# An adaLN block with windowed attention: each step made of two runs of small products and two of whole ones

## The chip, the cores and the metric

One core of one Trainium2 chip runs the whole kernel; the other cores do nothing. The metric is the device time of one execution in microseconds, and lower is better. The kernel before takes 1718.55 us (median of 3 runs, 1714.46 to 1723.47).

## What is computed

The input is 8 sequences of 256 tokens with 128 features. First comes one attention layer (8 heads of 16), and then, on its normalised and modulated output, six layers of the following, which are nearly all of the time:

```python
def attn_layer(x, Wqkv, qs, ksc, Wo):            # HEADS = 16, DIM_HEAD = 64, WINDOW = 32
    q, k, v = split(x @ Wqkv)                    # 128 -> 3 * 1024
    q = l2norm(q) * qs;  k = l2norm(k) * ksc
    q = q * cos * scale + rotate_half(q) * sin * scale
    k = k * cos * inv + rotate_half(k) * sin * inv
    # each window of 32 tokens attends to itself and to the window before it (64 keys), masked
    return local_attention(q, k, v) @ Wo         # 1024 -> 128
def ffn_layer(x, g, bln, W1, b1, W2, b2):        # hidden size 341
    xn = layernorm(x) * g + bln
    a, gate = split(xn @ W1 + b1)
    return a * gelu(gate) @ W2 + b2
for i in range(6):
    x = attn_layer(shift_tokens(x), ...) + x
    x = ffn_layer(shift_tokens(x), ...) + x
```

## The kernel before, in words

The six layers of eight sequences make 48 steps (`SLOTS`), one for each sequence of each layer. Every engine has its own program, an order written out by hand in a function `slot(g)` that it runs once for each step g; semaphores (`wait_ge` and `then_inc`) tie the engines together, and nothing reorders the work. A step's 256 tokens are two halves m = 0 and 1 of 128 tokens, and its 16 heads are two groups g = 0 and 1 of 8.

For one half the work goes round the engines so. TensorE projects Q, K and V (`q`, `k`, `v`; each six products of 128 x 128 by 512 columns, L717 to L721, with weights and input split in a high and a low part). VectorE multiplies Q and K with the tables (`rope_products`, L1420 and L1424), ScalarE squares them (`square_of`, L1063), VectorE sums the squares (`norms`, L1434), ScalarE makes the inverse norms (`inverse_norms`), GpSimd adds the two products (`rotate`, L406) and scales them (`scale`, L415). TensorE turns the result, that is, transposes it (`turn_q` and `turn_k`, 16 small products at L603 each), ScalarE copies it out of PSUM (`copy_q` and `copy_k`, L1081 and L1090), and TensorE makes the scores of each group (`scores`: 4 products at L760 for the mask and 64 at L767). VectorE subtracts the maximum (`centre`, L1445 and L1449), ScalarE takes the exponential (`exps`, L1104), TensorE turns P (`turn_p`), ScalarE copies it (`copy_p`, L1110), TensorE attends (`attend`, 64 products at L802 for a group), VectorE normalises (`normalise`, L1457 and L1460), TensorE turns the output (`turn_o`), ScalarE copies it (`copy_o`, L1119), and `project_out` (L824) is the product with Wo. V goes by `copy_v` (L1096) into `v_nat` and from there by eight DMAs of a half (`move_v`, L333), issued by SyncE, into the windows' places in `v_sb`; two more (`carry_v`, L343) carry the last window over. The feed-forward part of a sequence is done in the three steps behind it (`mean` L831, `variance` L836, gates and values at L846 to L848, `down` L885), with ScalarE's `gates` (L1154, between two table loads) and VectorE's `products` (L1486), `subtract_mean` (L1475) and `add` (L1494).

TensorE's products are of two kinds. The whole ones use all 128 rows and 128 columns of the array. The small ones use a part of it, by `tile_position`: the turns 64 x 128, the mask's 64 x 64, the scores and `attend` 64 x 32. PSUM has 8 banks of 512 floats, used here as four pairs (`pair_of_banks`), and each result lies in a pair until VectorE or ScalarE has read it, so that most of TensorE's waits are for a pair to come free. In the kernel before, P of a half is turned, copied and attended in the half-step of its own scores, with the copies of P group by group (`turn_p(g, 0, 0)`, `turn_p(g, 0, 1)`) and whole products put between them to cover what they wait for. So TensorE's step has eight runs of small products and eight of whole ones.

Steps 0 to 2 have no feed-forward part; steps 3 to 46 are a loop; step 47 and the rest of the last sequences are written out.

## Time and profile before

| what | value |
|---|---|
| time of the kernel before, median of 3 | 1718.55 us (1714.46 to 1723.47) |
| the profiled execution's own time | 1714.33 us |
| its span (first to last instruction) | 1712.5 us |
| busy: TensorE, VectorE, ScalarE, GpSimd | 1615.4, 1338.5, 1282.9, 1067.0 us |
| granted TensorE clock, mean over the span | 0.979 |
| steps 3 to 46, from the first scores of step 3 to those of step 47 (281.40 to 1649.10 us) | 1367.70 us |

The profile is of one execution. Busy time is the union of an engine's instructions, and matmuls overlap: one that takes 0.39 us is followed by the next after 0.23 us, so what a product costs is read as the distance from its start to the next one's start. In the timelines below, a row is a run of like instructions: start, time from its first start to its last end, engine, line, shapes and count; a bracket gives the idle time ahead of it and what ended it.

### The profile page before, as it was taken

Reading aid. Unit: us, or ns where it says so; the run is one execution under the profiler, and the core shown is the slowest. Engines: PE = TensorE matmul, PEld = TensorE weight load, DVE = VectorE, ACT = ScalarE, POOL = GpSimd, SP = SyncE. Lnnn points to the kernel's source line nnn. Section 1 sums busy time; section 2 is a strip of 40 time slices with the busy share of each in tenths; the row PEclk is TensorE's granted clock in tenths of the full one; section 3 lists DMA queues with packets and bytes.
Section 4 is the critical chain, followed back from the end, with each engine's and each line's share of the span. In section 5 each row is a group of like instructions: output and inputs, shape, how many; then the busy total and the mean of one; then the engine's idle time right before and its main releaser. Section 6 shows DMA issues by size and latency. Waiting matters only on the chain.

```text
span 1712.5 us, 89332 instructions
## 1 busy us (share of the span) xinstructions
PE 1615.4 (94%) x36892; PEld 1251.8 (73%) x36892; DVE 1338.5 (78%) x1952; ACT 1282.9 (75%) x2104; POOL 1067.0 (62%) x783
## 2 busy tenths in 40 slices
PE   7897688999999999999999999999999999999986
PEld 3575567777777777777777777777777777777765
DVE  5576767787888888888888888887887878888862
ACT  4795456788777778877778777778777787777763
POOL 2202556578666778667668667578676676676740
PEclk9898799999999999999999999999999999999998
DMA  3000323222323222324222324233223222232220
GB/s 119 2 0 1 73 59 105 62 66 61 91 70 93 70 69 68 85 55 116 68 57 63 88 69 112 51 72 80 72 66 103 70 70 70 69 73 69 71 48 26
DMA packets 75728, 116.79 MB, mean 68 GB/s; under 512 B 17294, under 2 KB 27276, under 8 KB 74764
## 3 DMA queue, kind: packets, MB, share of 16 engines
q1 hardware_dynamic: 75660, 115.99, 27.2%
q8 instruction: 30, 0.49, 0.1%
q14 instruction: 38, 0.31, 0.1%
HBM read 19.04 MB, written 1.05 MB: 12 GB/s over the span
## 4 chain that ended last, share of the span: by engine, by line
PE 89%; issue 5%; ACT 3%; DVE 2%; DMA 0%; ACTq 0%; DVEq 0%; SPq 0%
PE ps L603 15%; PE ps L824 10%; PE ps L717 10%; PE ps L802 9%; PE ps L767 9%; PE ps L721 8%; PE ps L720 8%; PE ps L885 4%; PE ps L760 3%; PE ps L846 2%; PE ps L847 2%; PE ps L848 2%; PE ps L836 2%; PE ps L831 2%; PE ps L592 1%
## 5 line engine op out<-in xcount | busy, mean ns | idle before, releaser
L415 POOL TENSOR_TENSOR arena<-arena,rnorm 128x1024 f32<-128x1024 f32 x192 | 361.9, 1906 | 342.7 <-ACT rnorm L1074 342.7
L406 POOL TENSOR_TENSOR arena<-arena 128x1024 f32<-128x1024 f32 x192 | 457.0, 2380 | 20.8 <-DVE arena L1424 17.9
L603 PEld LDWEIGHTS ps<-cst,arena 64*128 64x128 f32 x6656 | 243.5, 140 | 144.7 <-issue 136.0
L603 PE MATMUL ps<-cst,arena 64*128 64x64 f32 x6656 | 300.6, 230 | 21.6 <-ACT arena L1104 9.4
L1420 DVE TENSOR_TENSOR arena<-ps,rope 128x1024 f32<-128x1024 f32 x192 | 234.7, 1222 | 90.4 <-issue 81.5
L1110 ACT ACTIVATE arena<-ps 128x512 f32<-128x512 f32 x192 | 114.7, 597 | 174.4 <-PE ps L603 174.2
L1424 DVE TENSOR_TENSOR arena<-ps,rope 128x1024 f32<-128x1024 f32 x192 | 233.3, 1215 | 0.0
L721 PE MATMUL ps<-wqkv_hi,x_hi 128*128 128x512 f32 x576 | 230.1, 399 | 0.0
L720 PE MATMUL ps<-wqkv_lo,x_hi 128*128 128x512 f32 x576 | 229.2, 398 | 0.0
L717 PE MATMUL ps<-wqkv_hi,x_lo 128*128 128x512 f32 x576 | 215.7, 456 | 12.8 <-issue 11.6
L1434 DVE TENSOR_REDUCE norm<-arena 128x16 f32<-128x1024 f32 x192 | 224.3, 1209 | 0.0
L1445 DVE TENSOR_REDUCE rmax<-ps 128x8 f32<-128x512 f32 x192 | 131.9, 687 | 105.9 <-PE ps L767 105.3
L1063 ACT ACTIVATE arena<-ps 128x1024 f32<-128x1024 f32 x192 | 190.4, 1020 | 11.7 <-DVE arena L1424 11.7
L802 PE MATMUL ps<-v_sb,arena 64*32 64x66 f32 x12288 | 166.3, 227 | 23.1 <-issue 7.5
L824 PE MATMUL ps<-arena,wo_sb 128*128 128x256 f32 x768 | 186.3, 385 | 1.2 <-issue 1.2
L802 PEld LDWEIGHTS ps<-v_sb,arena 64*32 64x32 f32 x12288 | 138.6, 106 | 60.4 <-issue 50.0
L767 PE MATMUL ps<-k_t,arena 64*32 64x64 f32 x12288 | 166.2, 225 | 7.1 <-issue 7.1
L767 PEld LDWEIGHTS ps<-k_t,arena 64*32 64x32 f32 x12288 | 134.3, 106 | 31.1 <-issue 8.2
L824 PEld LDWEIGHTS ps<-arena,wo_sb 128*128 128x128 f32 x768 | 138.6, 190 | 19.7 <-issue 1.3
L1090 ACT ACTIVATE k_t<-ps 128x1024 f32<-128x1024 f32 x96 | 98.4, 1025 | 71.9 <-PE ps L603 70.1
L1449 DVE TENSOR_TENSOR arena<-ps,rmax 128x512 f32<-128x512 f32 x192 | 132.8, 692 | 15.2 <-DVE rmax L1445 0.7
L1460 DVE TENSOR_TENSOR arena<-ps,rden 128x512 f32<-128x512 f32 x192 | 132.9, 692 | 14.8
(122 smaller groups left out, 2752.3 us busy)
## 6 DMA issues: line engine op xcount, KB each, us to landing
v_sb<-v_nat SPq DMA_DIRECT2D x576, 130.0 KB, 2.4
v_sb<-v_nat SPq DMA_DIRECT2D x192, 65.0 KB, 2.0
wqkv_sb<-wqkv SPq DMA_DIRECT2D x6, 1536.0 KB, 6.4
v_sb<-v_sb SPq DMA_DIRECT2D x96, 65.0 KB, 2.0
wo_sb<-wo SPq DMA_DIRECT2D x6, 512.0 KB, 3.8
w_sb<-w SPq DMA_DIRECT2D x6, 341.0 KB, 3.0
x<-xT SPq DMA_DIRECT2D x1, 1024.0 KB, 5.0
scl<-scales SPq DMA_DIRECT2D x6, 128.0 KB, 6.2
```

What stands on the lines that cost most here:

```text
L406: pool.tensor_tensor(t_cos[:, m, j, :], t_cos[:, m, j, :], t_sin[:, j, :], ALU.add)\
L415: pool.tensor_tensor(x, x, rnorm[:, H * j:H * j + H].unsqueeze(2).to_broadcast([P, H, D]), ALU.mult).then_inc(s[done], 1)
L603: mm = pe.transpose(ps[0:width, bank + t, 64 * c:64 * c + 64], src[r], ident[r, r], tile_position=(64 * t, 0))
L717: pe.matmul(ps[:, bank + c, :], x_lo[:, m, :], wqkv_hi[:, w], start=True, stop=False)
L720: pe.matmul(ps[:, bank + c, :], x_hi[:, m, :], wqkv_lo[:, w], start=False, stop=False)
L721: mm = pe.matmul(ps[:, bank + c, :], x_hi[:, m, :], wqkv_hi[:, w], start=False, stop=True)
L767: mm = pe.matmul(ps[W * w:W * w + W, 4 * g + c, SPAN * hh:SPAN * hh + SPAN], q_t[r, 4 * g + hh, W * w:W * w + W], k_t[r, 4 * g + hh, P * m ...
L802: mm = pe.matmul(ps[W * w:W * w + W, 4 - 2 * g + c, ON * hh:ON * hh + ON], p_t[r, h, W * w:W * w + W], v_sb[r, m, w, VD * h:VD * h + ON], ...
L824: mm = pe.matmul(ps[:, 0, 0:N], wo_sb[:, c, :], o_t[:, c, :], start=(c == 0), stop=(c == H // 2 - 1), skip_group_check=True)
L1420: dve.tensor_tensor(t_cos[:, m, j, :].rearrange("p (h d) -> p h d", h=H), src.rearrange("p a (h d) -> p (a h) d", h=8), tc.unsqueeze(1).to ...
L1424: dve.tensor_tensor(t_sin[:, j, :].rearrange("p (h s d) -> p h s d", h=H, s=2), src.rearrange("p a (h s d) -> p (a h) s d", h=8, s=2)[:, : ...
L1434: dve.tensor_reduce(norm2[:, H * j:H * j + H], sq[:, j, :].rearrange("p (h d) -> p h d", h=H), AX.X, ALU.add).then_inc(s["normed"], 1)
```

## The change

Each of TensorE's steps becomes four runs: small, whole, small, whole. P is turned one half-step behind its scores and attended two behind: the small run at the head of step g holds `turn_q(g, 0)`, `attend(g - 1, 0, ...)`, `turn_k(g, 0)`, `turn_p(g - 1, 1)`, `scores(g, 0, ...)` and `turn_o(g - 1, 0)`. The run in the middle holds the same one half-step on. P of a half is turned in one piece (16 products for 2 times 8) and copied by one ScalarE instruction of 1024 columns for two of 512. The feed-forward part moves by a step at its head: mean and variance of sequence f are taken in step f + 2, not f + 1, while its gates stay in step f + 3. Every result has a new pair of banks (the tables `Q_PAIR` to `A_PAIR`), and with it new waits. ScalarE, VectorE, GpSimd and SyncE get new orders to match, and the head and the end of the pipeline are written anew. No product is added or removed.

The diff, cut to its core (of the slots of TensorE, ScalarE and VectorE only the lines of the new one are shown):

```diff
             def slot(g, norm=True, ahead=True, more=True, after=None, layer=None):
                 f = g - 2
-                if norm:
-                    divide(f)
                 scale(g, 1)
                 if ahead:
                     rotate(g + 1, 0, 0)
+                    low(g + 1, 1)
+                    rotate(g + 1, 0, 1)
                     if after == 7:
+                        table(layer, 1)
                         split_weights(layer, 2)
-                    low(g + 1, 1)
+                    scale(g + 1, 0)
+                    if after == 6:
+                        table(layer, 0)
                 if norm:
+                    divide(f)
                     scale_norm(f)
                 if ahead:
-                    rotate(g + 1, 0, 1)
-                    if after == 6:
-                        table(layer, 0)
-                    scale(g + 1, 0)
+                    rotate(g + 1, 1, 0)
                     if after == 6:
                         split_weights(layer, 0)
-                    rotate(g + 1, 1, 0)
-                    if after == 6:
-                        split_weights(layer, 1)
-                    if more:
-                        low(g + 2, 0)
                 if norm:
                     rest(f)
                 if ahead:
-                    rotate(g + 1, 1, 1)
-                    if after == 6:
-                        table(layer, 1)
                     if after == 2:
                         split_up(layer)
+                    if more:
+                        low(g + 2, 0)
+                    if after == 6:
+                        split_weights(layer, 1)
+                    rotate(g + 1, 1, 1)
...
+        Q_PAIR, K_PAIR, V_PAIR = (1, 0), (2, 3), (1, 0)
+        QT_PAIR, KT_PAIR, PT_PAIR, OT_PAIR = (1, 3), (2, 1), (2, 1), (3, 2)
+        S_PAIR = ((2, 0), (3, 1))
+        A_PAIR = ((0, 3), (0, 0))
...
+            def turn_k(pair, m, ff=True):
                 n = 2 * pair + m
                 pe.wait_ge(s["k_scaled"], CREDIT + n + 1)
+                if m == 0:
+                    pe.wait_ge(s["att_done"], CREDIT + pair - 1)
+                elif ff:
                     pe.wait_ge(s["f_prod"], CREDIT + 3 * (pair - LAG) + 3)
                 else:
+                    q_read(n + 1)
...
+            def turn_q(pair, m, ff=True):
                 n = 2 * pair + m
                 pe.wait_ge(s["q_scaled"], CREDIT + n + 1)
+                if m == 0:
+                    pe.wait_ge(s["v_copied"], CREDIT + n + 1)
+                elif ff:
+                    pe.wait_ge(s["f_gated"], CREDIT + 3 * (pair - LAG) + 3)
+                    pe.wait_ge(s["f_centred"], CREDIT + pair - 1)
+                else:
+                    pe.wait_ge(s["o_copied"], CREDIT + n - 2)
...
+            def attend(pair, m, g, bank=None):
                 n = 2 * pair + m
                 if g == 0:
                     pe.wait_ge(s["v_moved"], CREDIT + 16 * (18 * pair + 8 + 10 * m))
-                    pe.wait_ge(s["p_copied"], CREDIT + 2 * n + 2)
-                    pe.sem_inc(s["pe_waited"], 1)
-                elif over_q:
-                    pe.wait_ge(s["roped"], CREDIT + 4 * n + 10)
-                    pe.wait_ge(s["squared"], CREDIT + 2 * n + 5)
-                    pe.sem_inc(s["pe_waited"], 1)
+                    pe.wait_ge(s["p_copied"], CREDIT + n + 1)
+                if bank is None:
+                    bank = 2 * A_PAIR[m][g]
+                    if m:
+                        if g == 0:
+                            pe.wait_ge(s["v_copied"], CREDIT + n + 3)
+                        else:
+                            pe.wait_ge(s["o_normed"], CREDIT + 2 * n + 1)
+                    elif g == 0:
+                        q_read(n + 3)
+                        pe.wait_ge(s["f_done"], CREDIT + pair - 2)
+                    else:
+                        k_read(n + 3)
+                        pe.wait_ge(s["f_log"], CREDIT + pair - 1)
+                pe.sem_inc(s["pe_waited"], 1)
...
+            def slot(g, att=True, norm=True, ff=True, ahead=True):
+                turn_q(g, 0)
+                if att:
+                    attend(g - 1, 0, 0)
+                turn_k(g, 0)
+                if att:
+                    attend(g - 1, 0, 1)
+                    turn_p(g - 1, 1)
                 scores(g, 0, 0)
+                scores(g, 0, 1, att=att)
+                if att:
+                    turn_o(g - 1, 0)
                 if ahead:
                     q(g + 1, 0)
                 if ff:
+                    gates_01(g - LAG)
                 if ahead:
+                    k(g + 1, 0)
                 if ff:
+                    gate_2(g - LAG)
+                v(g, 1)
+                if ff:
+                    values(g - LAG, ahead)
+                if norm:
+                    pe.wait_ge(s["f_gated"], CREDIT + 3 * (g - LAG) + 3)
+                    mean(g - 2, 6)
+                if att:
+                    attend(g - 1, 1, 0)
+                turn_q(g, 1, ff)
+                turn_k(g, 1, ff)
+                turn_p(g, 0)
+                if att:
+                    attend(g - 1, 1, 1)
                 scores(g, 1, 0)
                 scores(g, 1, 1)
+                if att:
+                    turn_o(g - 1, 1)
                 if ahead:
+                    if not att:
+                        pe.wait_ge(s["v_copied"], CREDIT + 2 * g + 2)
                     q(g + 1, 1)
                     k(g + 1, 1)
+                    if norm:
+                        pe.wait_ge(s["centred"], CREDIT + 4 * g + 4)
+                        variance(g - 2, 2)
+                    if att:
+                        project_out(g - 1)
+                    if norm:
+                        pe.wait_ge(s["f_log"], CREDIT + g - 1)
+                    v(g + 1, 0)
+                    if ff:
+                        q_read(2 * g + 3)
+                        down(g - LAG)
...
+            def slot(g, att=True, shifted=True, norm=True, ff=True, ahead=True, more=True, after=None, layer=None):
+                copy_q(g, 0)
+                copy_k(g, 0)
+                if att:
+                    copy_p(g - 1, 1)
+                inverse_norms(g, 1)
+                if shifted:
+                    shift(g - 2)
+                if att:
+                    copy_o(g - 1, 0)
+                exps(g, 0, 0)
+                exps(g, 0, 1)
                 if ff:
                     act.preload_act_table_set("gelu_and_others")
+                    gate(g - LAG, 0, ps[:, 7, 0:N], 1)
+                    gate(g - LAG, 1, ps[:, 7, N:2 * N], 1)
+                if ahead:
+                    square_of(g + 1, 0, 0)
+                if ff:
+                    gate(g - LAG, 2, ps[:, 6, 0:N], 2)
+                copy_v(g, 1)
+                if ahead:
+                    high(g + 1, 1)
+                    square_of(g + 1, 0, 1)
+                copy_q(g, 1)
+                copy_k(g, 1)
+                copy_p(g, 0)
+                if ff:
                     act.preload_act_table_set("natural_log_exp_and_others")
                 if after == 7:
                     round_weights(layer, 2)
+                if att:
+                    copy_o(g - 1, 1)
                 if ahead:
                     inverse_norms(g + 1, 0)
                 exps(g, 1, 0)
                 if norm:
+                    square(g - 2)
+                exps(g, 1, 1)
                 if after == 6:
                     round_weights(layer, 0)
                 if after == 2:
                     round_up(layer)
                 if ahead:
                     square_of(g + 1, 1, 0)
+                    if norm:
+                        inverse_deviation(g - 2)
                     square_of(g + 1, 1, 1)
+                    if after == 6:
+                        round_weights(layer, 1)
+                    copy_v(g + 1, 0)
+                    if more:
+                        high(g + 2, 0)
+                    if norm:
+                        round_norm(g - 2)
...
+            def slot(g, att=True, norm=True, ff=True, ahead=True, first_mean=False):
+                if att:
+                    normalise(g - 1, 0, 0)
+                    normalise(g - 1, 0, 1)
                 centre(g, 0, 0)
                 centre(g, 0, 1)
                 if ahead:
                     rope_products(g + 1, 0, 0)
                     rope_products(g + 1, 0, 1)
                 if ff:
+                    product(g - LAG, 2, ps[:, 2, 0:N], 1)
+                if norm:
+                    subtract_mean(g - 2)
+                if ff:
+                    product(g - LAG, 0, ps[:, 3, 0:N], 2)
+                    product(g - LAG, 1, ps[:, 3, N:2 * N], 2)
+                if att:
+                    normalise(g - 1, 1, 0)
                 if ahead:
                     norms(g + 1, 0)
+                if att:
+                    normalise(g - 1, 1, 1)
                 centre(g, 1, 0)
                 centre(g, 1, 1)
                 if ahead:
                     rope_products(g + 1, 1, 0)
                     rope_products(g + 1, 1, 1)
+                    if att:
+                        residual(g - 1)
+                    if ff:
+                        add(g - LAG)
+                    if first_mean:
+                        subtract_mean(0, 5)
                     norms(g + 1, 1)
```

How the order moves on TensorE, in the loop over steps 3 to 46. Before, around the turning of P of the first half, there stood (L603 is a turn, L824 Wo's product, L846 a feed-forward product, and the other rows are instructions of the sequencer that wait or count):

```order
L777 ISA
L780 REGISTER_ALU [waits centred]
L603 MATMUL ps<-cst,arena 128x64 [waits exped]
L603 MATMUL ps<-cst,arena 128x64 x7
L824 MATMUL ps<-arena,wo_sb 128x256 x4
L603 MATMUL ps<-cst,arena 128x64 [waits p_copied,exped]
L603 MATMUL ps<-cst,arena 128x64 x7
L862 REGISTER_ALU
L846 MATMUL ps<-f_hi,w1_lo 128x256 [waits f_gated]
```

Each turn of a group of P stood between whole products. Now the head of the loop's step reads (L623 is a turn, L864 `attend`):

```order
L623 MATMUL ps<-cst,arena 128x64 [waits q_scaled,v_copied]
L623 MATMUL ps<-cst,arena 128x64 x15
L843 ISA
L844 ISA [waits v_moved]
L749 ISA [waits p_copied]
L750 ISA [waits roped]
L854 REGISTER_ALU [waits squared]
L864 MATMUL ps<-v_sb,arena 32x66 [waits f_done]
L864 MATMUL ps<-v_sb,arena 32x66 x31
```

The turn of Q and `attend` of the step before now follow each other, and `attend` has six semaphores to wait for. (One row of a fp32 product in these lists is two matmuls in the profile, except for the turns.)

On VectorE, in the loop, the rows around the middle of a step were the following before the change: `norms` (L1434) of the next step's first half behind `normalise` (L1457, L1460) of this one's.

```order
L1457 RECIPROCAL rden<-ps 128x8 [waits attended]
L1459 REGISTER_ALU [waits recip]
L1460 TENSOR_TENSOR arena<-ps,rden 128x2x4x64 [waits o_turned]
L1457 RECIPROCAL rden<-ps 128x8 [waits attended]
L1460 TENSOR_TENSOR arena<-ps,rden 128x2x4x64 [waits o_turned,recip]
L1432 REGISTER_ALU
L1433 REGISTER_ALU [waits squared]
L1434 TENSOR_REDUCE norm<-arena 128x16 [waits logged]
L1432 REGISTER_ALU
L1434 TENSOR_REDUCE norm<-arena 128x16 [waits logged,squared]
```

Now `norms` (L1533) stands between the two groups of `normalise` (L1557, L1560), and these are of the step before:

```order
L1557 RECIPROCAL rden<-ps 128x8 [waits attended]
L1559 REGISTER_ALU [waits recip]
L1560 TENSOR_TENSOR arena<-ps,rden 128x2x4x64 [waits o_turned]
L1531 REGISTER_ALU
L1532 REGISTER_ALU [waits squared]
L1533 TENSOR_REDUCE norm<-arena 128x16 [waits logged]
L1531 REGISTER_ALU
L1533 TENSOR_REDUCE norm<-arena 128x16 [waits logged,squared]
L1536 TENSOR_SCALAR norm<-norm 128x32 [waits normed]
L1553 REGISTER_ALU
L1557 RECIPROCAL rden<-ps 128x8 [waits attended]
L1560 TENSOR_TENSOR arena<-ps,rden 128x2x4x64 [waits o_turned,recip]
```

The second `normalise` of a half, which `turn_o` waits for, now has `norms` ahead of it, and `norms` waits for ScalarE's square of K.

## Rows read from the trace of the kernel before

**Rows 1.** The page: busy time of the engines, and the chain that ended last.

```profile
PE 1615.4 (94%) x36892; PEld 1251.8 (73%) x36892; DVE 1338.5 (78%) x1952; ACT 1282.9 (75%) x2104; POOL 1067.0 (62%) x783
...
PE 89%; issue 5%; ACT 3%; DVE 2%; DMA 0%; ACTq 0%; DVEq 0%; SPq 0%
```

**Rows 2.** Windows: length, then busy of PE, PEld, DVE, ACT, POOL, and PE's clock.

```profile
907.56:938.20 30.64, 30.42 (x740) 24.01 (x737) 25.29 (x36) 25.04 (x40) 27.29 (x20) 1.00 0.28 65
281.40:1649.10 1367.70, 1342.59 (x32388) 1057.83 (x32384) 1127.58 (x1585) 1076.62 (x1734) 956.12 (x690) 1.00 0.30 75
184.40:281.40 97.00, 82.18 (x2117) 63.94 (x2116) 71.42 (x94) 58.22 (x95) 59.42 (x41) 0.90 0.27 64
1649.10:1712.50 63.40, 42.48 (x764) 34.23 (x760) 20.97 (x44) 27.16 (x46) 9.06 (x10) 0.89 0.12 33
```

**Rows 3.** Timeline of TensorE over one step of the loop.

```profile
906.92 0.71 PE L603 MATMUL ps<-cst,arena 64*128 64x64 f32 x16
907.56 0.30 PE L760 MATMUL ps<-mask_bf,ident_bf 64*64 64x256 bf16 x4
...
909.68 0.73 PE L717 MATMUL ps<-wqkv_hi,x_lo 128*128 128x512 f32 x2
...
914.89 0.39 PE L720 MATMUL ps<-wqkv_lo,x_hi 128*128 128x512 f32 x1
915.12 0.40 PE L721 MATMUL ps<-wqkv_hi,x_hi 128*128 128x512 f32 x1
915.45 0.46 PE L603 MATMUL ps<-cst,arena 64*128 64x64 f32 x8
915.84 1.99 PE L824 MATMUL ps<-arena,wo_sb 128*128 128x256 f32 x8
917.76 0.46 PE L603 MATMUL ps<-cst,arena 64*128 64x64 f32 x8
918.15 0.39 PE L846 MATMUL ps<-f_hi,w_lo 128*128 128x256 f32 x1
918.37 0.28 PE L847 MATMUL ps<-f_lo,w_hi 128*128 128x256 f32 x1
918.49 0.28 PE L848 MATMUL ps<-f_hi,w_hi 128*128 128x256 f32 x1
...
919.41 1.72 PE L802 MATMUL ps<-v_sb,arena 64*32 64x66 f32 x128
921.06 1.20 PE L603 MATMUL ps<-cst,arena 64*128 64x64 f32 x32
922.19 0.74 PE L717 MATMUL ps<-wqkv_hi,x_lo 128*128 128x512 f32 x2
...
931.81 0.70 PE L831 MATMUL ps<-f_a,cst 128*128 128x256 f32 x2
932.62 1.82 PE L802 MATMUL ps<-v_sb,arena 64*32 64x66 f32 x128
```

**Rows 4.** Timeline of ScalarE: a table load, and two reads of 1024 columns.

```profile
910.01 1.28 ACT L1160 ACT_TABLE_LOAD   x1
...
918.76 1.94 ACT L1063 ACTIVATE arena<-ps 128x1024 f32<-128x1024 f32 x2
```

**Rows 5.** The same in step 11, where ScalarE's loop over layers turns back.

```profile
539.06 1.28 ACT L1160 ACT_TABLE_LOAD   x1 [2.47 <-issue]
```

**Rows 6.** VectorE over one step (the first is `rope_products`, the second `norms`).

```profile
L1420 DVE TENSOR_TENSOR arena<-ps,rope 128x1024 f32<-128x1024 f32 x4 | 4.9, 1222 | 1.8 <-issue 1.8
...
L1434 DVE TENSOR_REDUCE norm<-arena 128x16 f32<-128x1024 f32 x4 | 4.7, 1208 | 0.0
```

**Rows 7.** SyncE: eight issues of one `move_v`; then the page on their landing.

```profile
909.83 4.99 SPq L333 DMA_DIRECT2D v_sb<-v_nat  x8
...
v_sb<-v_nat SPq DMA_DIRECT2D x576, 130.0 KB, 2.4
```

**Rows 8.** TensorE in its loop's first pass, around a stop.

```profile
285.36 0.66 PE L767 MATMUL ps<-k_t,arena 64*32 64x64 f32 x30 [2.13 <-issue]
```

More of the change, by code:

```diff
@@ L958, in _ @@
+            mean(0, 5)
+            k_read(2 * LAG + 1)
+            variance(0, 6)
             with pe.Fori(LAG, SLOTS - 1) as g:
                 slot(pe.snap(g))
[L960 to L967 removed]
@@ new lines, in _ @@
+            project_out(g - 1)
+            pe.wait_ge(s["o_normed"], CREDIT + 4 * g + 1)
+            turn_p(g, 1, 6)
+            turn_o(g, 0, 2)
+            down(g - LAG)
+            pe.wait_ge(s["att_done"], CREDIT + g)
+            attend(g, 1, 0, 4)
+            attend(g, 1, 1, 6)
+            pe.wait_ge(s["f_done"], CREDIT + g - 2)
+            mean(g - 1, 1)
+            pe.wait_ge(s["f_log"], CREDIT + g - 1)
+            pe.wait_ge(s["o_copied"], CREDIT + 2 * g + 1)
+            last_up(g - 2)
@@ L975, in _ @@
+            turn_o(g, 1, 4)
+            variance(g - 1, 1)
+            project_out(g, 6)
+            down(g - 2, 7)
+            mean(g, 4)
+            variance(g, 4)
+            pe.wait_ge(s["f_log"], CREDIT + g)
+            last_up(g - 1)
+            pe.wait_ge(s["att_done"], CREDIT + g + 1)
+            last_up(g)
+            pe.wait_ge(s["f_done"], CREDIT + g - 1)
+            down(g - 1, 7)
+            pe.wait_ge(s["f_log"], CREDIT + g + 1)
+            down(g, 4)
         @block.scalar
```

455 lines of the change are left out of this document (196 added, 259 removed).

## The prediction

> **What bounds the kernel now.** The page comes first. TensorE is busy for 94% of the span, and the chain that ended last runs over it for 89%, with 5% more of "issue" [rows 1]. The windows say where: in steps 3 to 46, which take 1367.7 of the 1712.5 us, it is idle for 25.1 us in all, at a granted clock of 1.00 [rows 2]. The other engines have room: in the step from 907.56 to 938.20 us VectorE is busy for 25.3 of 30.64 us, ScalarE for 25.0 and GpSimd, in this one with weights to split, for 27.3 [rows 2]. So a step is worth what TensorE's products cost, start to start. The 44 steps would take 44 x 30.64 = 1348 at this length and take 1368. The 20 more are stops of about 2 us in the loop's first pass, of which one is shown [rows 8], and at ends of ScalarE's loops [rows 5]. Head and tail are another matter: TensorE is idle for 14.8 of the 97 us of steps 0 to 2 and for 21 of the last 63.4 us [rows 2].
>
> **What a change of kind costs.** The timeline of TensorE shows it to 0.01 us [rows 3]. Whole products follow each other after 0.23 us (914.89 to 915.12), but the last one before a turn holds 0.33 (915.12 to 915.45): 0.10 more. A whole product of the feed-forward part holds 0.12 (918.37 to 918.49), the first one behind a turn 0.22 (918.15 to 918.37): 0.10 more again. Eight turns take 0.39 (915.45 to 915.84) and 32 take 1.13 (921.06 to 922.19), so one costs 0.031 and each run of turns 0.14 on top. From one whole run to the next, over a run of turns, the fixed part is thus 0.34.
>
> **TensorE's new step.** Before, it has eight whole runs and eight blocks of turns (P's two, K's and Q's as one, the output's, for each half). Now it has two whole runs, and six blocks of turns: four in the first small run, where `attend` stands between them, and two in the second, where Q, K and P are turned side by side. The sum by difference: six whole runs fewer at 0.20 is 1.2, two blocks of turns fewer at 0.14 is 0.3. Besides, TensorE waits no more between `mean` and `attend` (931.81 to 932.62 is 0.81, where two of Wo's products and a change of kind cost 0.53), which gives 0.3. 30.64 - 1.8 = 28.85. The sum by parts agrees. A block of 16 turns is 0.14 + 16 x 0.031 = 0.64; a group of `attend` is half of 1.65 (919.41 to 921.06), 0.82; a half's scores are 2.12 (907.56 to 909.68). The first small run is 4 x 0.64 + 2 x 0.82 + 2.12 = 6.3, the second 0.82 + 1.62 + 0.82 + 2.12 + 0.64 = 6.0. Wo's products cost (1.92 - 0.20) / 8 = 0.215 each (915.84 to 917.76). The whole runs are 18 x 0.235 + 18 x 0.12 + 2 x 0.215 + 0.2 = 7.0 (Q, K, V, gates, values, mean) and 18 x 0.235 + 24 x 0.215 + 0.2 = 9.6 (Q, K, V, variance, Wo, down). Together 28.9.
>
> One thing speaks against so much. A block of 16 turns with the mask's products behind it takes 0.64 (906.92 to 907.56 [rows 3]), just what the slope and the 0.14 give for one with whole products behind it: for a run of turns the next small shape is as dear as a whole one. Counted by shape (turns, mask, scores and `attend`, whole), a step changes 26 times before and still 20 times now. The Trainium skill ("TensorEngine Tiling (Array Packing)", Key Properties) says that a change of the tiling mode, though not of the tile, drains TensorE; by that rule, with which the 0.64 agrees, a small run is no single piece and only the six fewer changes would count. The sum above goes by the rows; the other count is the first rival.
>
> **What TensorE will wait for.** I walk through a step, with t = 0 at `turn_q(g, 0)`. Reads of 1024 columns are 0.97 apart and end 1.02 after their start; a table load is 1.28 [rows 4]. The products with the tables take 2 x 1.14 for Q or K, the two sums of `norms` 2.4 [rows 6].
> - First small run, 0 to 6.3. The copy of K starts behind `turn_k` at 2.2 and ends at 3.2; the scores start at 3.56. Covered by 0.3. `attend(g - 1, 0, 0)` waits for `add`, which follows `down` of the step before: about 0.1.
> - First whole run, to 13.3. VectorE starts its step 3.1 late, since `add` and `norms(g, 1)` run over; it centres from 5.0 to 7.8 and multiplies Q by 10.2. ScalarE does the exponentials by 8.5, a table load, two gates, and the square of Q by 11.7; `values` waits for that at 11.8: 0.1.
> - Second small run, to 19.3. `mean` ends at 13.4, `subtract_mean` at 13.9, and both products of the feed-forward part at 14.7, which `turn_k(g, 1)` needs at 14.6: 0.1. ScalarE copies Q and K from 14.9 to 16.9, and the scores are due at 16.6: 0.2. `norms(g + 1, 0)` holds VectorE from 15.5 to 18.1, so `normalise(g - 1, 1, 1)` ends at 19.1, and `turn_o(g - 1, 1)` is due at 18.8: 0.3.
> - Second whole run, 9.6 long: VectorE multiplies K by 26.3, ScalarE squares it by 27.4, and `copy_v(g + 1, 0)` is done when `down` is. Nothing.
> That is 0.7 to 0.8, and the step 29.65. GpSimd, in this walk, scales K of a half 6 us before its turn. The V moves: eight issues take 5.0 and land 2.4 later [rows 7]; those of half 0 start at 3.0, land at 10.5 and are needed at 11.9.
>
> The gain of a step is 30.64 - 29.65 = 1.0, and 44 steps give 44. Bounds: no wait at all gives 1.8 and 79; waits of twice what I find give 0.25 and 11.
>
> **Head, tail and the stops.** Steps 0 to 2 take 97.0 us [rows 2], latency for the most part, since there P goes round within its half-step. The new step 0 attends nothing, and in steps 1 and 2 the round trips lie behind other work; VectorE then sets the pace with some 24 us of work. I take 26.3, 26.5 and 26.5, and add 2.1 for a stop and 2 for mean and variance of sequence 0, which stand by themselves: 83.4, and 14 gained (bounds 0, if code loading takes the gain, and 20). The tail is a chain through every engine, the same from the last scores on. It has more straight code, one `attend` of 256 matmuls more, hence one stop of 2 more; on the other side the last scores come about 5 earlier. I take 3 gained (bounds -6 and 8). The 2.47 us at ScalarE's loop end [rows 5] now delay the copies of Q and K with 0.3 of cover; four of these cost some 1.6 to 2.2 each, as now, and the rounding of weights is better hidden: 2 gained.
>
> The sum is 44 + 14 + 3 + 2 = 63. Against the profiled execution's own 1714.3 this is 1651; the median of the plain runs stands 4 above it, and I put the forecast between, at 1653.
>
> **Rivals.**
> - Every change of shape costs alike. The fixed 0.34 of a round trip over turns is two changes, 0.17 each; six fewer are 1.0 and the wait 0.3, 1.3 for 1.8. With my waits 0.55 a step is left, 24, and with head and tail 1714 - 43 = 1671. Against it: the 0.20 of a whole run is seen at the whole products themselves, and they are what goes. Chance 0.1. (This is the case of the Trainium skill's tiling page, Key Properties.)
> - More waits of the kind that I found, two or three tenths in several places, since the covers are thin: 1.5 a step, 0.3 gained, 1714 - 13 - 19 = 1682. Chance 0.15.
> - No change: the waits take all of 1.8, and the head gives little. 1706 to 1722. Chance 0.06.
> - Slower, by one mechanism: the DMAs of V. `copy_v(g, 1)` needs all eight DMAs of half 0 landed, and in ScalarE's order the square of K and the copies of Q and K stand behind it, for which the second scores wait. They now start only after `attend(g - 1, 0, 1)`. With 1.4 of slack, each further us of landing is one of TensorE's. At 7.4 us from first issue to last landing it is hidden; beyond 8.8 it costs, and from about 10.2 on it has used up step and head (1.0 + 19 / 44 = 1.4). At 12 the step is 32.85, 2.2 longer than now: 1714 + 97 - 19 = 1792. For it speaks that the queue is shared with the weights; against it that the median landing is 2.4 [rows 7]. Chance 0.07.
> - Almost no waits, 28.9 to 29.2 a step: about 1620. Chance 0.1.
>
> **How the numbers follow.** My forecast, a step of 29.2 to 30.0 us, 1635 to 1671, has 0.52. The range takes in its bounds, the almost free case and the two of less gain: 1620 to 1692 holds 0.82. Within 0.5% (about what a measurement of this kernel can tell from no change) is 1710 to 1727. Faster by more has 0.52 + 0.1 + 0.15 + 0.1 = 0.87, less 0.01 for the edge; the same has 0.06, slower 0.07 and the 0.01 of the other edge.
>
> **What would show it.** In the new timeline the step of the loop is 29.65 long; the last whole product of a run still holds 0.33, the first 0.10 too much, twice a step each; the four waits are found at `values`, `turn_k(g, 1)`, the second scores and `turn_o(g - 1, 1)`, none over 0.5; scores of step 3 start near 266 us. The prediction is wrong if the boundary inside a small run (turn to `attend`, six semaphores to read) costs more than a turn's 0.14, if the granted clock, 1.00 in steps 3 to 46 and 0.90 in steps 0 to 2 with their gaps [rows 2], falls in the longer small runs, or if a wait of over 1 us stands in the step.

## The result, and the profile after

The changed kernel takes 1738.8 us (1737.7 to 1743.0), the kernel before 1717.6 (1714.5 to 1723.5): ratio 1.0124, interval 1.0091 to 1.0156. It is slower by 1.2%, where I forecast 1653. The page of after, its head, the busy times and the chain:

```profile
span 1741.1 us, 89711 instructions
PE 1578.5 (91%) x36892; PEld 1278.8 (73%) x36892; DVE 1380.0 (79%) x1952; ACT 1284.1 (74%) x2008; POOL 1070.1 (61%) x783
...
PE 76%; issue 10%; DVE 10%; ACT 3%; DVEq 1%; DMA 0%; POOL 0%; ACTq 0%; SPq 0%; POOLq 0%
```

TensorE's share of the chain fell from 89% to 76%, and VectorE, with 2% before [rows 1], has 10%. The windows of after answer to [rows 2]: one step, steps 3 to 46, steps 0 to 2, and the part from the first scores of step 47 on.

```profile
979.80:1011.08 31.28, 29.49 (x739) 24.43 (x736) 26.82 (x37) 24.22 (x37) 20.59 (x16) 1.00 0.27 64
281.04:1667.49 1386.45, 1307.76 (x32384) 1082.95 (x32385) 1165.99 (x1582) 1078.32 (x1646) 958.33 (x688) 0.99 0.29 72
183.04:281.04 98.00, 77.26 (x1953) 61.70 (x1954) 71.86 (x91) 54.27 (x83) 60.12 (x41) 0.90 0.28 73
1667.49:1741.05 73.56, 50.58 (x934) 41.60 (x930) 24.09 (x52) 30.91 (x51) 9.78 (x11) 0.82 0.16 43
```

TensorE's own work in steps 3 to 46 did fall, from 1342.6 to 1307.8 us busy. But it is idle for 78.7 us there, where it was for 25.1. The list of its waits names the new one:

```profile
PE ps L808 <- DVE arena L1560: 40.1, 33, 1.3
...
PE ps L864 <- DVE h L1590: 9.2, 44, 0.3
```

The second scores of half 0 (those of its second group of heads; L808 is their mask) wait 33 times, 1.2 us each, for VectorE's `normalise(g - 1, 0, 0)`. The timelines of VectorE and GpSimd at a step's end say why that is late (the last two rows are the masks of the first and the second scores):

```profile
1007.41 0.48 DVE L1590 SCALAR_TENSOR_TENSOR h<-ps,par,h 128x256 f32 x1 [2.26 <-PE ps L947]
1007.81 2.34 DVE L1533 TENSOR_REDUCE norm<-arena 128x16 f32<-128x1024 f32 x2
1010.18 2.17 DVE L1536 TENSOR_SCALAR norm<-norm 128x32 f32<-128x32 f32 x1
1012.27 0.20 DVE L1557 RECIPROCAL rden<-ps 128x8 f32<-128x8 f32 x1
1012.59 0.69 DVE L1560 TENSOR_TENSOR arena<-ps,rden 128x512 f32<-128x512 f32 x1
...
1009.39 0.41 POOL L418 TENSOR_TENSOR x_lo<-h,x_hi 64x128 fp32r<-64x128 f32 x1 [0.18 <-POOL x_lo L415]
1009.96 2.36 POOL L425 TENSOR_TENSOR arena<-arena 128x1024 f32<-128x1024 f32 x1 [0.16 <-POOL x_lo L418]
...
1011.08 0.30 PE L808 MATMUL ps<-mask_bf,ident_bf 64*64 64x256 bf16 x4
1013.43 0.30 PE L808 MATMUL ps<-mask_bf,ident_bf 64*64 64x256 bf16 x4 [1.25 <-DVE arena L1560]
```

L1536 is the floor of the norms, a maximum over 32 columns, the last instruction of `norms`. It lasts 2.17 us, and the same instruction lasts 0.18 elsewhere. GpSimd's sum of K's two parts (L425) begins 0.22 earlier and ends at 1012.32; the floor ends at 1012.35. The record shows no idle time at all: the hold is inside a duration. A shorter hold was in the trace of before as well:

```profile
937.76 0.33 DVE L1437 TENSOR_SCALAR norm<-norm 128x32 f32<-128x32 f32 x1
939.33 0.69 DVE L1445 TENSOR_REDUCE rmax<-ps 128x8 f32<-128x512 f32 x1 [1.24 <-PE ps L767]
...
937.31 0.75 POOL L442 TENSOR_TENSOR f_a<-f_a 128x256 f32<-128x256 f32 x1
```

There the floor ends at 938.09, GpSimd's product at 938.06, and what follows on VectorE waits for scores until 939.33 anyway. The change put a longer instruction of GpSimd at this place, and behind the floor two operations that TensorE waits for. The Trainium skill ("SBUF — State Buffer", Who interferes with whom) says that VectorE and GpSimd share a pair of ports, which whoever starts first has for its whole instruction, and that a `tensor_scalar` can need it while a `tensor_reduce` does not. The rows agree: the two sums before the floor keep their 1.2 us each beside GpSimd's work, and the floor is held to the end of GpSimd's sum.

The hold is not in every step, and after shows by itself what it costs. Ahead of steps 11, 27 and 43 the floor lasts 0.26 to 0.27, and these steps are 29.9 to 30.0 long (19 and 35, behind a floor of 0.27, take 31.1 and 31.2, and 31.0 in the first kernel below, which has no floor at all); ahead of steps 7, 15, 23, 31 and 39 it lasts about 0.6, and they are 30.4 to 30.7; where it lasts 2.1 to 2.2, most are 31.2 to 31.4.

### The profile page after: what moved, and what is told of

The parts are those of the page before. It is cut to its first block, busy times and chain, and to the rows that moved or that the text cites. A ratio compares the mean times of both kernels' runs of the same rounds, so it can differ in the third digit from the quotient of the medians.

```text
span 1741.1 us, 89711 instructions
## 1 busy us (share of the span) xinstructions
PE 1578.5 (91%) x36892; PEld 1278.8 (73%) x36892; DVE 1380.0 (79%) x1952; ACT 1284.1 (74%) x2008; POOL 1070.1 (61%) x783
## 4 chain that ended last, share of the span: by engine, by line
PE 76%; issue 10%; DVE 10%; ACT 3%; DVEq 1%; DMA 0%; POOL 0%; ACTq 0%; SPq 0%; POOLq 0%
PE ps L623 10%; PE ps L888 10%; PE ps L740 9%; PE ps L743 8%; PE ps L744 8%; PE ps L815 7%; DVE norm L1533 5%; PE ps L864 5%; PE ps L947 3%; PE ps L903 3%; PE ps L808 2%; PE ps L905 2%; PE ps L904 2%; DVE arena L1560 2%; PE ps L612 1%
## 5 line engine op out<-in xcount | busy, mean ns | idle before, releaser
L425 POOL TENSOR_TENSOR arena<-arena 128x1024 f32<-128x1024 f32 x192 | 456.2, 2376 | 136.3 <-DVE arena L1523 122.5
L623 PE MATMUL ps<-cst,arena 64*128 64x64 f32 x6656 | 291.0, 230 | 45.7 <-issue 13.9
L623 PEld LDWEIGHTS ps<-cst,arena 64*128 64x128 f32 x6656 | 249.3, 140 | 103.1 <-issue 89.3
L1148 ACT ACTIVATE arena<-ps 128x1024 f32<-128x1024 f32 x192 | 196.9, 1026 | 102.4 <-DVE arena L1523 101.3
L1533 DVE TENSOR_REDUCE norm<-arena 128x16 f32<-128x1024 f32 x192 | 224.5, 1210 | 0.2 <-ACT arena L1148 0.2
L740 PE MATMUL ps<-wqkv_hi,x_lo 128*128 128x512 f32 x576 | 204.7, 437 | 0.6 <-issue 0.6
L864 PE MATMUL ps<-v_sb,arena 64*32 64x66 f32 x12288 | 166.7, 227 | 14.3 <-DVE h L1590 9.2
L888 PE MATMUL ps<-arena,wo_sb 128*128 128x256 f32 x768 | 175.7, 382 | 1.4 <-ACT arena L1204 1.4
L815 PE MATMUL ps<-k_t,arena 64*32 64x64 f32 x12288 | 170.1, 229 | 6.7 <-issue 6.6
L1204 ACT ACTIVATE arena<-ps 128x1024 f32<-128x1024 f32 x96 | 98.5, 1026 | 99.3 <-PE ps L623 99.2
L864 PEld LDWEIGHTS ps<-v_sb,arena 64*32 64x32 f32 x12288 | 136.4, 106 | 42.6 <-issue 36.0
L888 PEld LDWEIGHTS ps<-arena,wo_sb 128*128 128x128 f32 x768 | 147.0, 192 | 22.5 <-ACT arena L1204 1.9
L815 PEld LDWEIGHTS ps<-k_t,arena 64*32 64x32 f32 x12288 | 137.5, 107 | 31.4 <-issue 9.2
L1560 DVE TENSOR_TENSOR arena<-ps,rden 128x512 f32<-128x512 f32 x192 | 132.8, 692 | 14.4
L1166 ACT ACTIVATE arena<-ps 128x1024 f32<-128x1024 f32 x96 | 98.4, 1025 | 45.7 <-PE ps L623 34.0
```

What stands on the lines that cost most here:

```text
L425: pool.tensor_tensor(t_cos[:, m, j, :], t_cos[:, m, j, :], t_sin[:, j, :], ALU.add)\
L623: mm = pe.transpose(ps[0:width, bank + t, 64 * c:64 * c + 64], src[r], ident[r, r], tile_position=(64 * t, 0))
L740: pe.matmul(ps[:, bank + c, :], x_lo[:, m, :], wqkv_hi[:, w], start=True, stop=False)
L815: mm = pe.matmul(ps[W * w:W * w + W, bank + c, SPAN * hh:SPAN * hh + SPAN], q_t[r, 4 * g + hh, W * w:W * w + W], k_t[r, 4 * g + hh, P * m ...
L864: mm = pe.matmul(ps[W * w:W * w + W, bank + c, ON * hh:ON * hh + ON], p_t[r, h, W * w:W * w + W], v_sb[r, m, w, VD * h:VD * h + ON], start ...
L888: mm = pe.matmul(ps[:, bank, 0:N], wo_sb[:, c, :], o_t[:, c, :], start=(c == 0), stop=(c == H // 2 - 1), skip_group_check=True)
```

## The experiments

Each was compared with the kernel before on its chip; the ratios are to it. Where a step's length or a distance between starts is given, it is taken start to start in the trace. In the diffs `...` marks lines left out. All kernels but `x2_sum_waits` and `x9_sum_earlier` are without the floor, by the first diff, which is not shown again.

**Floor taken out** (`x1_no_floor`). Only a norm of nearly zero would come out otherwise.

```
-                dve.wait_ge(s["normed"], CREDIT + 2 * n + 2)
-                dve.tensor_scalar(norm2[:, :], norm2[:, :], 1e-24, None, ALU.max).then_inc(s["guarded"], 1)
...
-                act.wait_ge(s["guarded"], CREDIT + n + 1)
-                act.activation(norml[:, :], norm2[:, :], ACT.Ln, scale=2.0 ** 24)...
+                act.wait_ge(s["normed"], CREDIT + 2 * n + 2)
+                act.activation(norml[:, :], norm2[:, :], ACT.Ln, scale=2.0 ** 24, bias=2.0 ** 24 * 1e-24)...
```

> The changed kernel without VectorE's floor of the norms (a maximum over 32 columns, the last instruction of VectorE's loop); ScalarE's Ln gets 1e-24 as a bias instead. In 35 of 45 steps of after this instruction lasts 2.1 to 2.2 us instead of 0.18, and ends together with a sum of GpSimd's that began 0.2 us before it (1009.96 to 1012.32 there, 1010.18 to 1012.35 here). Theory H, held off by GpSimd: the instruction waits for GpSimd's sum to end, both normalise operations and the second scores of the step stand behind it, and the step is 31.3 instead of 29.9. Without it nothing holds VectorE: the wait of 1.2 before the second scores goes, a step is 29.9 to 30.1, 35 x 1.4 = 49 are gained: 1690 (1684 to 1700). Rival L, the end of VectorE's loop: its branch costs 2 us before the next instruction can start, and the record of the last one is stretched over it. Then the 2 us appear between the last sum of norms and the first reciprocal, and the time is 1737 to 1741. Rival D, VectorE simply has too much to do behind add: a gain of 0.2 a step, 1732.

Measured: 1688.0 us, ratio 0.9857 (0.9838 to 0.9875). The step is 29.90. VectorE and TensorE of this kernel at the same place:

```profile
977.96 2.34 DVE L1534 TENSOR_REDUCE norm<-arena 128x16 f32<-128x1024 f32 x2
980.22 0.20 DVE L1556 RECIPROCAL rden<-ps 128x8 f32<-128x8 f32 x1
...
981.24 0.30 PE L808 MATMUL ps<-mask_bf,ident_bf 64*64 64x256 bf16 x4
981.47 0.86 PE L815 MATMUL ps<-k_t,arena 64*32 64x64 f32 x64
982.26 0.30 PE L808 MATMUL ps<-mask_bf,ident_bf 64*64 64x256 bf16 x4
```

The reciprocal follows the sums at once, across the same loop end, so the 2 us were not that end (rival L falls), and the second mask starts 1.02 behind the first, where in after it was 2.35. The floors of over 2 us are 33 in after's loop and not the 35 that I had counted.

**The floor kept, GpSimd's sum behind it** (`x2_sum_waits`).

```
+                    pool.wait_ge(s["guarded"], CREDIT + 2 * g + 4)
                     rotate(g + 1, 1, 1)
```

> The changed kernel with one wait more: GpSimd begins its last sum of a step (cosine and sine part of K) only once VectorE has done the floor of the norms. The floor stays where it is, and no work is left out. Theory H: in after GpSimd's sum starts 0.2 us ahead of the floor; now it starts about 0.3 us later, after it, and the floor lasts 0.18 again. Gain as without the floor, less a little: 1690 to 1702, steps of 29.9 to 30.2. Rival L (end of VectorE's loop): nothing changes for VectorE, 1739 or slower. Rival D (too much work): 1739 too.

Measured: 1691.5 us, ratio 0.9892 (0.9865 to 0.9919), steps of 29.9 to 30.0.

```profile
980.02 0.18 DVE L1537 TENSOR_SCALAR norm<-norm 128x32 f32<-128x32 f32 x1
...
980.37 2.36 POOL L425 TENSOR_TENSOR arena<-arena 128x1024 f32<-128x1024 f32 x1 [0.73 <-DVE norm L1537]
```

One wait more, on an engine with room, and nothing left out: the floor is back at 0.18, and 47 us are gone. VectorE has the same instructions in the same order as in after, so rival D falls too.

**GpSimd's sum earlier** (`x9_sum_earlier`), a smaller hold.

```
                     rotate(g + 1, 1, 0)
+                    if more:
+                        low(g + 2, 0)
+                    rotate(g + 1, 1, 1)
...
                     rest(f)
-                    if more:
-                        low(g + 2, 0)
...
-                    rotate(g + 1, 1, 1)
```

> The changed kernel with the floor, and with GpSimd's last sum of a step put ahead of rest(f); the lower part of x stays ahead of it. Nothing is added or left out. The sum, 2.36 long, then begins about 1.2 us earlier in after's times (1008.8 instead of 1009.96) and ends at 1011.2, while the floor still begins at 1010.2. Theory H (VectorE's floor is held until GpSimd's sum ends): the floor lasts 1.0 to 1.2 instead of 2.17. A hold of 2.0 cost 1.4 a step, so some 0.6 are covered; a hold of 0.9 costs 0.3 to 0.4, a step is 30.2 to 30.4, and 35 x 1.0 are gained: 1704 (1696 to 1712). Rival L (the end of VectorE's loop): 1739, and the floor stays at 2.1 to 2.2.

Measured: 1707.3 us, ratio 0.9959 (0.9945 to 0.9973).

```profile
991.61 1.23 DVE L1536 TENSOR_SCALAR norm<-norm 128x32 f32<-128x32 f32 x1
...
990.43 2.37 POOL L425 TENSOR_TENSOR arena<-arena 128x1024 f32<-128x1024 f32 x1 [0.16 <-POOL x_lo L418]
```

With the floor at 0.18, 1.23 and 2.17 us a step is 29.9, 30.4 and 31.3. So the step follows the length of the hold, as theory H has it.

**The kernel before without the floor** (`x3_before_no_floor`), with the diff of the first.

> The kernel before, without the floor in the same way. There the floor takes 0.33 to 0.66 us in most steps and 1.47 in each eighth, but VectorE's next work is a maximum over scores that TensorE delivers only 1.2 us later. Theory H: no gain, 1716 to 1719: the hold of GpSimd was there before, hidden behind the wait for the scores, and the change has brought it on the path. If the floor cost something before too, it is at most 5 x (1.47 - 1.2) = 1.4 us.

Measured: 1715.0 us, ratio 1.0009 (0.9996 to 1.0022), steps of 30.7 as before. The hold was hidden.

**An extra whole run** (`x7_extra_boundary`).

```
-                if att:
+                if att and not ahead:
                     turn_o(g - 1, 1)
...
                     q(g + 1, 1)
+                    if att:
+                        turn_o(g - 1, 1)
```

> The changed kernel without the floor, and with one block of 16 turns (the output of half 1) moved from the end of the second small run into the whole run behind it, after Q's products. The number of blocks of turns stays, one whole run more is made. By the prediction's price a whole run's boundaries cost 0.20: 44 x 0.20 = 9 us more than x1_no_floor, 1697. By the price of the first rival (every change of shape 0.17) nearly the same, 7.5. If boundaries cost nothing, 1688. What it could add by itself: the copy of this block on ScalarE comes 1.9 later, and with it the exponentials of half 1; if that reaches TensorE, it is more than 15.

Measured: 1741.7 us, ratio 1.0138 (1.0110 to 1.0166): 54 more than `x1_no_floor`, not 9. A step is 1.48 longer.

```profile
1001.75 0.40 PE L744 MATMUL ps<-wqkv_hi,x_hi 128*128 128x512 f32 x1
1002.08 0.71 PE L623 MATMUL ps<-cst,arena 64*128 64x64 f32 x16
1002.72 0.73 PE L740 MATMUL ps<-wqkv_hi,x_lo 128*128 128x512 f32 x2
...
1003.99 0.39 PE L744 MATMUL ps<-wqkv_hi,x_hi 128*128 128x512 f32 x1
1005.35 0.67 PE L898 MATMUL ps<-f_a,cst 128*128 128x256 f32 x2 [0.96 <-ACT f_a L1220]
...
1002.83 1.02 ACT L1207 ACTIVATE arena<-ps 128x1024 f32<-128x1024 f32 x1 [2.20 <-PE ps L623]
...
1004.80 0.40 ACT L1220 ACTIVATE f_a<-f_a 128x256 f32<-128x256 f32 x1
```

The boundaries cost 0.30: 0.10 before the block (1001.75 to 1002.08), 0.11 behind it, and 0.09 where scores now meet a whole product. The other 1.2 is one wait: `variance` (L898) waits for a square on ScalarE (L1220), which stands behind the copy of the moved block (L1207). By the term that it was made to test it should have been 9. The expectation had named the late copy as what could make it more than 15, and had not priced it; so the total says nothing on the boundaries, and only the distances between starts do.

**Turns of Q and K side by side** (`x5_turns_together`).

```
                 turn_q(g, 0)
+                turn_k(g, 0)
                 if att:
                     attend(g - 1, 0, 0)
-                turn_k(g, 0)
-                if att:
                     attend(g - 1, 0, 1)
```

> The changed kernel without the floor, with TensorE's turns of Q and K side by side in the first small run: turn_q, turn_k, attend, attend, turn_p in place of turn_q, attend, turn_k, attend, turn_p. No work is added or left out. In x1_no_floor a step is 29.90, and TensorE's starts show 0.12 more at a turn followed by attend, 0.135 more at attend followed by a turn, and a further 0.27 at the first attend (it waits for add, behind down of the step before). Theory W (the step is TensorE's work and a few small waits): the wait for add goes, since the turn of K lies before it, and two changes of kind go, less 0.08 for the step from Q's turns to K's: 0.4 to 0.5 a step, 44 x 0.45 = 20, so 1668 (1664 to 1674). Rival V (VectorE sets the step behind add): its first normalise starts no earlier, and the time stays at 1686 to 1690.

Measured: 1674.4 us, ratio 0.9772 (0.9731 to 0.9813), a step of 29.63: 0.27 gained where 0.45 was expected. The small run in `x1_no_floor`, and then here:

```profile
977.28 0.71 PE L623 MATMUL ps<-cst,arena 64*128 64x64 f32 x16
978.19 0.85 PE L864 MATMUL ps<-v_sb,arena 64*32 64x66 f32 x64 [0.20 <-DVE h L1589]
978.98 0.71 PE L623 MATMUL ps<-cst,arena 64*128 64x64 f32 x16
979.62 0.86 PE L864 MATMUL ps<-v_sb,arena 64*32 64x66 f32 x64
980.59 0.72 PE L623 MATMUL ps<-cst,arena 64*128 64x64 f32 x16
```

```profile
972.28 1.21 PE L623 MATMUL ps<-cst,arena 64*128 64x64 f32 x32
973.42 1.80 PE L864 MATMUL ps<-v_sb,arena 64*32 64x66 f32 x128
975.33 0.71 PE L623 MATMUL ps<-cst,arena 64*128 64x64 f32 x16
```

The two blocks of turns and the first wait went from 0.91 + 0.64 to 1.14, as said. But the two groups of `attend` take 1.91 from their start to the next turn, where 0.79 and 0.98 stood: the 0.14 that the turns gain beyond the wait of 0.27 is lost again at the joint of two groups of the same shape. Two changes of shape fewer gained nothing in sum.

**The straight parts.** Five kernels change only head or tail: `x4_head_order` has V's copy ahead of K's square in steps 0 to 2, on the kernel without the floor; `x6_both_orders` has the same on `x5_turns_together`; `x10_first_norm` puts the norm of sequence 0 into step 2, also on `x5_turns_together`; `x8_tail_order` has `variance` behind the first `attend` of step 47, on the kernel without the floor, and `x11_best` has that on `x10_first_norm`. First `x4_head_order`:

```
+                    if not ff:
+                        copy_v(g + 1, 0)
                     square_of(g + 1, 1, 1)
...
-                    copy_v(g + 1, 0)
+                    if ff:
+                        copy_v(g + 1, 0)
```

> The changed kernel without the floor, and in steps 0 to 2 alone ScalarE copies V of the next step ahead of the square of K (in after it stands behind it). In these steps TensorE has no products of Wo and down, and its first turn of a step waits for this copy: 3.83 us at 209.49, 1.17 at 244.95, 2.58 at 280.17. Theory, the head is set by this chain (product of K with the tables on VectorE, its square, the copy of V, the turn of Q): 1.0 to 1.4 us earlier in each of three steps, 3 to 4 us less than the kernel without the floor. Rival, the head is set by loading code (the page puts these waits down to issue): no difference between the two.

Measured: 1684.5 us, ratio 0.9862 (0.9819 to 0.9905). Here and in `x1_no_floor` the first turn of step 1 starts 0.1 behind the copy of V, and TensorE's stop ahead of it fell from 3.99 to 1.74. Steps 0 and 1 fell from 30.45 to 28.10 and from 34.87 to 33.48, and step 2 rose from 32.30 to 34.07. The scores of step 3 come 2.6 earlier, 0.7 of it from ahead of step 0; the total can't be told from `x1_no_floor`.

The same on the other order, `x6_both_orders`:

> The order of x5_turns_together, and the order of ScalarE's copy of V in steps 0 to 2 of x4_head_order. If the two add up, 3 to 4 us less than x5_turns_together: 1665. If step 2 gives back what step 0 gains, as scores of step 3 only 2.6 earlier in x4_head_order say, 1 to 3 less.

Measured: 1676.7 us, ratio 0.9774 (0.9750 to 0.9798). The stop ahead of the first turn of step 1 fell here too, from 3.66 to 1.52, but steps 0 to 2 take 98.5 where they took 98.0 in `x5_turns_together`: nothing is left of the 3 us.

The norm of sequence 0, `x10_first_norm` (TensorE's part; the other engines' orders of step 2 change with it):

```
...
-            with pe.Fori(1, LAG) as g:
-                slot(pe.snap(g), norm=False, ff=False)
-            mean(0, 5)
-            k_read(2 * LAG + 1)
-            variance(0, 6)
+            slot(1, norm=False, ff=False)
+            slot(2, ff=False)
...
```

> As x5_turns_together, and the norm of sequence 0 is made inside step 2, as in every later step, in place of by itself behind step 2 (steps 1 and 2 of TensorE are written out for it). In x1_no_floor variance(0) waits 1.74 for its square at 274.44, and mean, variance and this wait stand alone: about 3 us of the 97.6 of the head. If the head is what its open waits and its work add up to, scores of step 3 come 2.5 to 3.5 earlier, at 277.5 to 278.5, and the time is 1671. If the first turns then wait for VectorE instead (scores of step 3 at 280 or later, as in x6_both_orders), 1674.

Measured: 1676.3 us, ratio 0.9776 (0.9756 to 0.9796). It misses its 1671, and neither of its two cases came: steps 0 to 2 take 103.5 instead of 98.0, and step 3 takes 33.4 instead of 36.2. With the steps written out, TensorE's stops of 1 to 2 us that the trace puts down to "issue" stand in steps 1 and 2 (1.97 at 267.54, 1.94 at 284.86), and fewer in step 3 than in `x5_turns_together`. `x11_best` has the same head and takes 100.2.

The tail, `x8_tail_order`:

```
-            variance(g - 2, 0)
             pe.wait_ge(s["centred"], CREDIT + 4 * g + 3)
             attend(g, 0, 0, 6)
+            variance(g - 2, 0)
```

> The changed kernel without the floor; in the straight part behind the last step alone the first attend of step 47 stands before the variance of sequence 45, for whose square TensorE waits 2.0 us at the end of the last small run. The attend needs only P, long turned, and the centring of the scores just made. If the part behind the last scores is bound by TensorE's order, 0.8 to 1.2 us less than x1_no_floor: 1687. If its chain runs over the exponentials and the turn of P (3 us later), nothing: 1688. A difference this small may not be told from none in the total; the start of the turn of P in the trace tells it.

Measured: 1688.3 us, ratio 0.9830 (0.9801 to 0.9860). From the last scores to the turn of P behind them it is 10.4 us, and 10.7 without the order: no gain that the total shows.

And `x11_best`, with both:

> As x10_first_norm, with the order of x8_tail_order in the part behind the last step. 0 to 1 us less than x10_first_norm: 1670 to 1671, ratio to before 0.974.

Measured: 1674.7 us, ratio 0.9759 (0.9733 to 0.9784). It can't be told from `x5_turns_together`, which has less in it. Both beat the kernel before by 2.3 to 2.4%, and by the ratios the changed kernel by 3.5 to 3.6%. Both are without the floor; the order of `x5_turns_together` with the floor kept and GpSimd made to wait was not run.

## Why the prediction was wrong

In the loop the change does nearly what I said, and that is lost by one instruction, which my walk had left out. Without it the kernel takes 1688.0 us, which is still 35 above the forecast: head and tail gained nothing. By parts, in us of the span (steps by their first scores):

| | before | forecast | after | no floor |
|---|---|---|---|---|
| up to step 0 | 184.4 | 184.4 | 183.0 | 183.8 |
| steps 0 to 2 | 97.1 | 83.4 | 98.0 | 97.6 |
| step 3 | 37.0 | | 41.6 | 36.8 |
| steps 4 to 46 | 1330.7 | | 1344.8 | 1297.3 |
| steps 3 to 46 | 1367.7 | 1321.7 | 1386.4 | 1334.1 |
| from step 47 | 63.4 | 60.4 | 73.6 | 69.4 |
| whole span | 1712.5 | 1649.9 | 1741.1 | 1684.9 |

- **The step that failed** is the walk's first item: "VectorE starts its step 3.1 late, since `add` and `norms(g, 1)` run over". With t = 0 at 1007.13, the sums of `norms` end at 1010.15, 3.0 later, where I had 3.1. VectorE then starts its step at 1012.27, 5.1 late. I had priced `norms` by its two sums [rows 6] and left out its third instruction. I looked at GpSimd only for what it delivers ("GpSimd, in this walk, scales K of a half 6 us before its turn"), and never for what it holds. Shown by the three lengths of the hold, of which the one at 0.18 has the floor kept, and by the kernel before, where the same instruction costs nothing. Worth 1344.8 - 1297.3 = 47.5 us, of 91 between the forecast's span and after's. It is also the wait of over 1 us that I had named as a sign of being wrong; the other two did not come (a turn with `attend` behind it costs no more than I had, and the granted clock is 1.00 in the step and 0.99 over steps 3 to 46).
- **TensorE's new step**: right, within 0.1. Without the floor the four runs take 6.63, 7.14, 6.50 and 9.61, 29.9 in all, where I had 6.3, 7.0, 6.0 and 9.6 without waits. The waits below make up the difference. Scores take 2.04 where I had 2.12, and a group of `attend` 0.79 where I had 0.82; 48 turns side by side take 1.85 where I had 1.63, since 0.14 and 0.09 pass at the joints of Q's, K's and P's turns, which I had for free. 16 turns with `attend` behind them take 0.64, as I had it. An extra whole run costs 0.30 (`x7_extra_boundary`), where I had 0.20. The rival by which every change of shape costs alike is not borne out: the joints of blocks of one shape (0.14 and 0.09) cost about as much as that from turns to `attend` (0.15), and in `x5_turns_together` two changes fewer gained nothing in sum. What passes at a joint stays open.

```profile
961.18 0.87 PE L864 MATMUL ps<-v_sb,arena 64*32 64x66 f32 x64
962.13 1.92 PE L623 MATMUL ps<-cst,arena 64*128 64x64 f32 x48
963.97 0.86 PE L864 MATMUL ps<-v_sb,arena 64*32 64x66 f32 x64
965.00 0.30 PE L808 MATMUL ps<-mask_bf,ident_bf 64*64 64x256 bf16 x4 [0.16 <-issue]
```

- **The waits**: 0.7 to 0.8 forecast, 1.0 found: attend for `add` 0.27, turn of P 0.18, turn of Q 0.15 (961.18 to 962.13 is 0.95 for a group of 0.79), scores of half 1 0.23, and about 0.17 at `values`. The step is 29.90 where I had 29.65, so this term, the waits, was 0.25 too small: 44 x 0.25 = 11 us. `turn_o(g - 1, 1)` shows no wait in most steps, and a turn of P takes its place. The waits behind an `attend` (0.08 to 0.16 of idle) come with no engine late in the trace; what they are stays open.
- **Head**: "The new step 0 attends nothing, and in steps 1 and 2 the round trips lie behind other work" failed. I took 26.3 to 26.5 a step, and they take 32.0, 33.7 and 32.3. TensorE's work fell (77.3 busy, 82.2 before), and its idle time rose from 14.8 to 20.7. VectorE's work was 24.0 a step, as said, but it idles for 26 us, so it does not set the pace. One link is the chain of K's product, its square, V's copy and the turn of Q: `x4_head_order` and `x6_both_orders` shorten its wait by some 2 us, and the next steps give it back in part or whole. Which chain sets steps 1 and 2 is not settled. Worth 14.6 us.
- **Tail**: "the last scores come about 5 earlier" failed. From the first scores of step 47 to the last it is 16.5 and 18.2 us in the two traces of the old order, 20.0 to 22.9 in nine of the new one, and 18.2 and 15.2 in `x11_best` and `x10_first_norm`. More work is not the reason: up to the mask of the last scores TensorE is busy for 11.5 us in `x10_first_norm`, at a granted clock of 1.00, and for 13.9 in before. What fills the time are stops that the trace puts down to "issue", 6.9 us in after and 2.0 in before, and the clock, 0.85 in after and 1.00 in before. The forecast had one such stop of 2 for all of it. What the stops are stays open. From the last scores on, the old order takes 46.9 and 48.6, seven kernels of the new one without the hold 46.1 to 48.5, which is the same, as said; but `x9_sum_earlier` takes 49.3, and `x10_first_norm`, `x11_best` and after take 53.3, 50.7 and 50.7, at a clock of 0.78 to 0.81. Worth 13 us in after, and 9 without the floor.
- **First pass of the loop**: 41.6 in after and 36.8 without the floor. In after's step 3 whole products start 0.43 apart in two stretches instead of 0.23, behind stops of 1.5 and 1.8 us; the mean granted clock is 0.75, and 0.91 without the floor. Of kernels that begin alike one had 0.79 and took 39.9 (`x8_tail_order`), and others had 0.91 to 0.95, so these 5 us may be chance.
- **The rivals**: the one on the slower side was the wrong one. No wait in after's list of waits is for V's DMAs. None of my cases has GpSimd in it, and 0.08 for slower was too little for a schedule with covers of 0.2 to 0.3.

## What to carry to other kernels

An order of work changes which instructions of VectorE and GpSimd run at the same time, and here a short `tensor_scalar` that began behind a long `tensor_tensor` of GpSimd's lasted until that one's end: look, in the trace of before, for instructions of one shape whose duration differs (here 0.18, 0.33 and 1.47), and ask who will stand beside and behind them afterwards. A wait inside a duration shows in no list of waits; the spread of a line's durations gives it away (the floor before: 0.18 at least, 0.19 in the middle, 1.48 at most). If such a pair is found, try one semaphore that lets the short one go first, where the long one has room: here the step is 29.95 with it, and 29.9 with the floor gone.

## What was unexpected of the hardware

A maximum over 128 x 32 numbers took 2.17 us instead of 0.18, to within 0.03 us of the end of GpSimd's 2.36 us sum. The line of the floor in four kernels (busy us, mean ns):

```profile
L1437 DVE TENSOR_SCALAR norm<-norm 128x32 f32<-128x32 f32 x96 | 39.5, 411 | 3.3
```

```profile
L1536 DVE TENSOR_SCALAR norm<-norm 128x32 f32<-128x32 f32 x96 | 91.2, 950 | 3.3
```

```profile
L1536 DVE TENSOR_SCALAR norm<-norm 128x32 f32<-128x32 f32 x96 | 66.2, 689 | 3.3
```

```profile
L1537 DVE TENSOR_SCALAR norm<-norm 128x32 f32<-128x32 f32 x96 | 23.8, 248 | 3.3
```

They are before, after, `x9_sum_earlier` and `x2_sum_waits`. After spends 52 us more in this one line than before. Its loop loses 47.5 us by it, and without the line the changed kernel is 25 us faster than the kernel before (1688.0 and 1713.3 on one chip).
